# The token products of y on 128 columns of the array in place of 64

## What is computed

```python
x = x + base0(x) + lora0[adapter0](x)      # 512x512 weights, rank 16
x = x + base1(x) + lora1[adapter1](x)      # 512x512 weights, rank 16
w = L2_weights[subjects]                   # 64x64 for each batch
x = x + jnp.einsum('bct,bcd->bdt', x, w)
w = L3_weights[conditions]                 # 64x64 for each batch
x = x + jnp.einsum('bct,bcd->bdt', x, w)
```

## Time and profile before

| | us |
|---|---|
| median of 3 runs | 170.71 |
| lowest and highest run | 169.84, 171.48 |
| the profiled execution | 169.73 |
| its span, first to last instruction | 168.0 |
| TensorE busy in it | 160.4 (95%) |
| VectorE, ScalarE, GpSimd busy | 92.9, 47.0, 57.2 |

### The profile page before, as it was taken

The page is one execution under the profiler, slowest core; times in us unless marked ns, Lnnn a source line. Parts: engine busy times, 40 slices in busy tenths (PEclk is TensorE's granted clock), DMA queues, the critical chain, the costliest instruction groups (busy, mean ns, idle before and its releaser), DMA issues.

```text
span 168.0 us, 6390 instructions
## 1 busy us (share of the span) xinstructions
PE 160.4 (95%) x2365; PEld 124.9 (74%) x2365; DVE 92.9 (55%) x220; ACT 47.0 (28%) x90; POOL 57.2 (34%) x167
## 2 busy tenths in 40 slices
PE   5899999999989979999999999999999999999992
PEld 5678748758776848887888687788778886877782
DVE  4967766889757382348534842693386355423010
ACT  3234225481206202330332032221402420422110
POOL 4341110446750358007701840481067007500000
PEclk9999999999999999999999999999999999999999
DMA  4999786449577997308633833492177321333123
GB/s 149 302 342 325 226 228 214 129 161 329 162 234 241 307 342 245 127 29 258 219 125 124 277 100 125 165 303 114 44 265 234 125 98 47 111 125 129 62 79 108
DMA packets 21947, 30.79 MB, mean 183 GB/s; under 512 B 7272, under 2 KB 9704, under 8 KB 21928
## 3 DMA queue, kind: packets, MB, share of 16 engines
q1 hardware_dynamic: 20320, 25.31, 44.8%
q0 software_dynamic: 1600, 5.24, 10.7%
q10 hardware_dynamic: 8, 0.00, 0.0%
HBM read 19.80 MB, written 10.75 MB: 182 GB/s over the span
## 4 chain that ended last, share of the span: by engine, by line
PE 93%; DMA 3%; issue 1%; SPq 1%; POOL 0%; ACT 0%
PE o_ps L853 68%; PE y_ps L853 21%; DMA w_sb<-in_L_cond_W_dram 3%; PE y_ps L937 1%; PE y_ps L866 1%; PE y_ps L906 1%; PE y_ps L950 0%; SPq L250 0%; POOL w_sb L406 0%; SPq L253 0%; PE y_ps L981 0%; ACT o_sb L560 0%
## 5 line engine op out<-in xcount | busy, mean ns | idle before, releaser
L853 PE MATMUL o_ps<-g,yy 128*128 128x512 f32 (+1 forms) x384 | 89.0, 389 | 0.0
L853 PEld LDWEIGHTS o_ps<-g,yy 128*128 128x128 f32 x384 | 70.5, 188 | 20.3 <-issue 5.3
L392 POOL COPY u_sel<-u_tab 128x64 f32 x128 | 32.2, 271 | 61.8 <-PE o_ps L853 42.6
L723 DVE TENSOR_TENSOR yy<-y_all,yy 128x512 fp32r<-128x512 f32 x32 | 22.1, 697 | 27.0 <-ACT yy L483 26.8
L483 ACT ACTIVATE yy<-y_all 128x512 fp32r<-128x512 f32 x32 | 20.1, 629 | 52.1 <-issue 23.8
L763 DVE COPY o_sb<-o_ps 128x512 f32<-128x512 f32 x15 | 10.4, 691 | 22.4 <-PE o_ps L853 22.4
L716 DVE COPY y_all<-y_ps 128x512 f32<-128x512 f32 x32 | 19.9, 682 | 4.3 <-PE y_ps L853 4.3
L380 POOL DMA_INDIRECT v_sel<-v_table,v_rows x16 | 15.3, 959 | 11.1 <-PE o_ps L853 8.4
L853 PE MATMUL y_ps<-p_now,x_raw 64*64 64x64 f32 x1024 | 17.6, 220 | 0.9 <-issue 0.9
L853 PEld LDWEIGHTS y_ps<-p_now,x_raw 64*64 64x64 f32 x1024 | 16.1, 135 | 2.3 <-issue 1.7
L515 ACT ACTIVATE o_sb<-o_ps 128x512 f32<-128x512 f32 x16 | 9.4, 591 | 21.5 <-PE o_ps L853 17.6
(11 more groups left out here) (119 smaller groups left out, 110.2 us busy)
## 6 DMA issues: line engine op xcount, KB each, us to landing
x_raw<-in_x_dram SPq DMA_DIRECT2D x16, 512.0 KB
out_dram<-o_sb SPq DMA_DIRECT2D x14, 512.0 KB, 3.1
w_sb<-in_L_cond_W_dram SPq DMA_DIRECT2D x4, 256.0 KB, 5.0
wb_sb<-in_L_cond_W_base_dram SPq DMA_DIRECT2D x4, 256.0 KB, 5.1
wp_sb<-in_L_cond_Wp_dram SPq DMA_DIRECT2D x2, 512.0 KB, 6.8
wt_sb<-in_L_cond_Wt_dram SPq DMA_DIRECT2D x1, 1024.0 KB, 10.6
w_of<-w_pick SPq DMA_DIRECT2D x4, 256.0 KB, 3.5
w_all<-w_of SPq DMA_DIRECT2D x4, 256.0 KB, 5.9
```

The costliest lines, as they stand in the source:

```text
L392: nc.gpsimd.tensor_copy(u_sel[2 * h + u][:, :, b, RANK * part:RANK * part + RANK], u_tab[:, :, bass.ds(e, 1), :].rearrange("p k a r -> p k ...
L723: nc.vector.tensor_tensor(yy[u][:, :, 1, :], y_all[u][:, :, :], yy[u][:, :, 0, :].bitcast(F32), ALU.subtract).then_inc(yl_set, 1)
L853: return nc.tensor.matmul(dst, lhsT, rhs, start=start, stop=stop)
```

## The change

The inner loop of `mix` ran over two halves of each 128-channel block. Now one product takes the whole block: the stationary operand is 64 rows x 128 columns and the result has all 128 partitions. A batch's rows are one half of the array's rows, as before. The columns of `y_ps` that are written and the values are the same.

```diff
                 for u in range(2 * h, 2 * h + 2):
                     for k in range(KC):
-                        for half in range(2):
-                            to = slice(SEQ * half, SEQ * half + SEQ)
-                            col = D // 2 * (u % 2) + SEQ * k
-                            d = PART * k + SEQ * half
-                            for b in range(2):
-                                rows = slice(SEQ * b, SEQ * b + SEQ)
-                                last = mm(y_ps[to, 2 * h + b, col:col + SEQ], x_raw[rows, u, d:d + SEQ], p_now[rows, u, :],
-                                          True, True)
+                        col = D // 2 * (u % 2) + SEQ * k
+                        for b in range(2):
+                            rows = slice(SEQ * b, SEQ * b + SEQ)
+                            last = mm(y_ps[:, 2 * h + b, col:col + SEQ], x_raw[rows, u, PART * k:PART * k + PART],
+                                      p_now[rows, u, :], True, True)
                     last.then_inc(y_done, 1)
```

## The result

| | before | after |
|---|---|---|
| median (runs) | 170.28 (4) | 181.36 (4) |
| lowest to highest | 169.18 to 171.48 | 180.97 to 181.66 |
| span of the profiled execution | 168.0 | 179.9 |

The ratio is 1.0634, 95% interval 1.0588 to 1.068: 6.3% slower, where 183.1 us and 7.3% were forecast, in the range of 180.5 to 186.5 us. In a later comparison the kernel before had a median of 170.67 us over 17 runs. Ratios here are of fast runs alone: a run over 1.5% above the fastest of the same kernel counts as slow and is left out of them, though not out of the medians.

A forecast was written before the change was run, and what follows sets the result against it. TensorE was taken as the bound: wider loads add 13.6 us over eight quads, a vanished gather wait returns 1.15, so 169.73 becomes 182.2; 0.98 from profiled run to median gives 183.1 us, range 180.5 to 186.5.

The follow-up runs named there:

- quarters: The kernel before, whose token products of y each use a quarter of the array (64 rows x 64 stationary columns); median 170.28 us.
- turns of 8: The changed kernel with its products reordered: for each pair, four of one row half, then four of the other; 187.06 us.
- turns of 16 records: The changed kernel with its products reordered: all eight of one row half, then all eight of the other; 223.64 us.
- eighths: The kernel before with each mix product cut once more, 128 products of 64x32 a quad; 189.45 us.
- half a pass on both halves: The changed kernel with only 32 of 64 moving columns in each token product of y, half of y not computed; 183.71 us.

## What to carry to other kernels

A stationary operand that is used for few moving columns is paid by its load, so compare the load's columns with the pass before you make a product wider: here in f32 64 columns of each were level, and at 128 the load alone counted. Merging two products that already run side by side on the array saves nothing by itself; it would pay only if the wide load then served 128 moving columns, which cost 0.05 us a mix more, and little even then: 3.77 us against 2 x 2.02 = 4.04 for quarters used twice, an estimate that no run checked. Price such a change by the spacing of starts between neighbours that differ in one size, not by busy time. And read every idle piece called "issue" against the code and the landings of DMAs before you call it a stop of the engine: here the long ones in front of `reduce` and `add_v` were waits for data.

## What the runs showed that had not been expected

- TensorE does not keep to the order of the program between row halves. With turns of 8 and of 16 records (0.50 and 1.39 us) the other half starts some four records before this one is through. The Trainium skill ("TensorE: Matmul & The Clock Gate", Part 3, "The mechanism") has matmuls in strict order from start to end. The turns of these two runs are 0.40 us too short for that.
- Records can follow each other at 10.4 ns each over 256 of them.
- TensorE can stop for up to 3.5 us in code on its first run. In ten such stops it went on 1.1 to 1.7 us after a packet of instructions had landed.
- The granted clock fell from 2.4 to 1.2 GHz for a while behind seven of the eight longest stops in these traces (1.84 to 3.51 us), though not behind eighths' first one, of 1.96 us. The work behind them is then slower: 13.76 us of applied products in place of 12.15 with eighths, at a mean of 0.88, after the stop of 3.51 us.
- It fell also with TensorE at work all the time. In turns of 16 records it stood at 1.00 for three turns of quad 1's mix and at a mean of 0.55 in the fourth. In turns of 8 (the row halves in turn) and in the changed kernel it stayed at 1.00. With half a pass on both halves it fell twice.
